# TensorE's order within a slot: the key score ahead of the max score, and the turn of the outputs between them

## The chip, the cores and the metric

One core of a Trainium2 chip runs the whole program. The metric is the device time of one execution in microseconds: 1221.77 us before the change (median of three runs, 1220.28 to 1222.41). Lower is better.

## What is computed

The input is `x`, 8 sequences of 512 tokens with 256 features, float32. Four layers follow each other, each added to its own input:

```
x = x + attn_a(layernorm(x))     # 16 heads of 16, biases, softmax over all 512 keys
x = x + ffn(layernorm(x))        # query, 255 router gates, products along a tree to 256 leaves, leaf values, output
x = x + attn_b(layernorm(x))     # 16 heads of 16, rotary positions, causal softmax
x = x + ffn(layernorm(x))
```

In both attentions `scores = q @ k.T / sqrt(16)`, `softmax(scores) @ v`, and a projection back to 256 features. Every score is wanted twice: once to find the largest of each query's row, and once, less that largest, to be exponentiated.

## The kernel before the change

The work is cut into 16 **phases**: one attention with the feed-forward network behind it, of one of the 8 sequences. Phases 0, 1, 2, 4, 6, 8, 10 and 12 are of `attn_a` ("plain"), phases 3, 5, 7, 9, 11 and 13 to 15 of `attn_b` ("causal"). A phase has 64 **slots**, four for each of 16 steps: a step is a group of four heads and one of four tiles of 128 keys. All engines walk through the same list of slots, and the order on each engine is written out by the program; only semaphores tie them together.

In each slot TensorE (`core` of the tensor block) does this:

- `ahead` calls `scores` (line 1082), the **max score**: 128 queries of one head against its keys (512 in a plain phase; 128, 256, 384 or 512 in a causal one) into one of three banks `ps_max`. It is for the unit that stands 28 slots (LEAD) further on, so that from slot 36 of a phase it belongs to the next phase. VectorE (`largest`, line 842 in a plain phase, 838 in a causal one) reduces the bank to `neg_max`. The max score waits until VectorE has done the reduction three units back, whose bank it takes. The first unit of a phase waits also for the DMAs that stack q and k.
- In slots 9, 25, 41 and 57, `turn_out` (line 1138) transposes the finished output of four heads, four times 128x128, and VectorE (`divide`, lines 863 and 866) divides it by the sums, behind that slot's reduction.
- `by_key` (line 1104), the **key score**: 128 keys against the queries (512, or fewer in a causal phase), with one more row that subtracts the maximum, into one of two banks `ps_key`. ScalarE takes the exponential (line 750). The key score waits until the exponential two slots back is done.
- In every fourth slot `mixed` (line 1128) multiplies the probabilities of four heads with the values, some five slots behind their exponentials. In causal phases GpSimd masks them first (line 655).
- Behind `core` stand the steps due in that slot (`matmul_schedule`): transposes (line 1183) and products (lines 1212 and 1237) of the previous phase's end and of the next phase's start.

VectorE's program goes slot by slot in the same way: first the reduction, then `divide` if there is one, then the steps due (normalisation, line 968; the gates' tree `leaves`, lines 990 to 999; values with bias, line 1045; residual additions, line 900). ScalarE does an exponential per slot, and then its steps. In the first eight slots of phase 0 two max scores are due in each slot (`lead_slots`). Each engine starts its instructions in program order, so one that waits holds all behind it.

The part that the change touches is `core`, with the functions that it calls:

Of the kernel before, what the change touches and what calls it, by code (L numbers as in the profile page):

```python
# [150 lines left out]
def causal(n):  # L151

    return n >= PHASES - AHEAD or (n >= AHEAD and n % 2 == AHEAD % 2)
# [62 lines left out]
def lead_slots(n, slot):  # L216

    if n == 0 and slot < CATCH_UP:
        return 2 * slot - CATCH_UP, 2 * slot - CATCH_UP + 1
    return slot,  # L220
# [24 lines left out]
def out_due(n, slot):  # L245

    if slot % GROUP_SLOTS == (GROUP_SLOTS - GROUP + TURN_LAG) % GROUP_SLOTS and (n > 0 or slot >= TURN_LAG):
        return (slot // GROUP_SLOTS - (1 if TURN_LAG >= GROUP else 0)) % GROUPS
    return None


def work_banks():


    uses = [(step, i, 0, -1) for step, i in PREPARE_FIRST if step in BANK_STEPS]
    for n in range(PHASES + 1):
        for slot in range(-LEAD if n == 0 else 0, SLOTS if n < PHASES else 0):
            if slot >= 0:
                if out_due(n, slot) is not None:
                    uses.append(("turn_out", n, slot))  # L260
                uses += [(step, i, m, n) for step, i, m, part in matmul_schedule(n).get(slot, ()) if part == 0]
    uses.append(("turn_out", PHASES, 0))
    uses += [(step, i, PHASES - 1, PHASES) for step, i in FINISH_LAST if step in BANK_STEPS]
    return {use: at % 2 for at, use in enumerate(uses)}
# [24 lines left out]
def build(nc, x, w, out):  # L289
    with ExitStack() as ctx:  # L290
# [82 lines left out]
        bank_of = {use: ps_work[i] for use, i in work_banks().items()}  # L373
# [681 lines left out]
        def _(pe):  # L1055
            count = Count()
            def take(bank, event):

                if bank.name in count.last_read:
                    read, n = count.last_read[bank.name]  # L1060
                    pe.wait_ge(on[read], count.of(read, count.n[read] - n))
                count.add(event)
                count.last_read[bank.name] = event, count.n[event]
# [21 lines left out]
            def ahead(n, slot):  # L1085
                n, unit, g, j, qt = score_unit(n, slot)
                if n < PHASES:
                    scores(n, unit, g, j, qt)

            def by_key(n, slot):  # L1090
                step, j = slot // GROUP, slot % GROUP
                g, kb = step // TILES, step % TILES
                q0 = P * kb if causal(n) else 0
                if kb == 0 and j == 0:
                    sent = on["shift_sent0"] if g % 2 == 0 else on["shift_sent1"]

                    count.add(f"shift_sent{g % 2}", BLOCKS)
                    pe.wait_ge(sent, count.of(f"shift_sent{g % 2}") * DMA)

                if count.some("exp_done", 1):  # L1100
                    pe.wait_ge(on["exp_done"], count.of("exp_done", 1))
                count.add("exp_done")
                h = GROUP * g + j
                pe.matmul(ps_key[slot % 2][:, 0:T - q0], k_stack[n % 2][0:STACK_ROWS, h, P * kb:P * kb + P],  # L1104
                          q_stack[n % 2][0:STACK_ROWS, h, q0:T], start=True, stop=True).then_inc(on["keyed_full"], 1)

            def mixed(n, step, begun):


                g, kb = step // TILES, step % TILES  # L1110
                q0 = P * kb if causal(n) else 0
                if causal(n):

                    pe.wait_ge(on["causal_done"], count.next("causal_done"))
                else:

                    pe.wait_ge(on["exp_done"], count.of("exp_done", begun))
                if step == 0:

                    pe.wait_ge(on["values_ready"], count.of("values_ready"))  # L1120
                if kb == 0:

                    if count.some("out_ready"):
                        pe.wait_ge(on["out_ready"], count.of("out_ready"))
                    count.add("out_ready")
                for j in range(GROUP):
                    at = VALUE * (HEADS * kb + GROUP * g + j)
                    last = pe.matmul(ps_out[COLS * j:COLS * j + COLS, q0:T], v_flat[n % 2][:, at:at + COLS],  # L1128
                                     probs[step % RING][:, j, q0:T], start=(kb == 0), stop=(kb == TILES - 1),
                                     tile_position=(0, COLS * j))  # L1130
                last.then_inc(on["mixed_done"], 1)

            def turn_out(g, begun, bank):

                pe.wait_ge(on["out_ready"], count.of("out_ready", begun))
                take(bank, "attended")
                for qt in range(TILES):
                    last = pe.transpose(bank[:, P * qt:P * qt + P], out_raw[g % 2][:, P * qt:P * qt + P], ident[:, :])
                last.then_inc(on["out_turned"], 1)

            def core(n, slot):
                for at in lead_slots(n, slot):
                    ahead(n, at)
                if out_due(n, slot) is not None:
                    turn_out(out_due(n, slot), 1, bank_of["turn_out", n, slot])
                by_key(n, slot)
                if slot % GROUP == MIX_LAG % GROUP:
                    step = (slot - MIX_LAG) // GROUP
                    if step >= 0:
                        mixed(n, step, MIX_LAG - GROUP + 1)  # L1150
                    elif n > 0:
                        mixed(n - 1, step + STEPS, MIX_LAG - GROUP + 1)
# [98 lines left out]
            for n in range(PHASES):  # L1251
                due = matmul_schedule(n)
                for slot in range(SLOTS):
                    core(n, slot)
                    for step, i, m, part in due.get(slot, ()):
                        steps[step](m, i, n, bank_of[step, i, m, n], (part,))
# [48 lines left out]
```

## Time and profile before

| | |
|---|---|
| time of the runs, median (lowest to highest) | 1221.77 us (1220.28 to 1222.41) |
| the profiled execution's own time | 1224.61 us |
| its span in the trace | 1222.9 us |
| TensorE matmul busy | 1112.1 us, 91% of the span |
| VectorE busy | 927.2 us, 76% |
| ScalarE busy | 720.2 us, 59% |
| GpSimd busy | 302.7 us, 25% |
| mean granted clock of TensorE | 0.957 of full speed |

Busy time of TensorE is modelled at its ends and matmuls overlap, so the distance from one start to the next tells what a matmul costs in a dense stream. Idle time stands beside an instruction with the engine that ended it, and the chain of waits follows the last instruction back to what released it at each step.

### The profile page before, as it was taken

How to read it: one execution, taken by the hardware profiler on the slowest of the kernel's cores; microseconds unless marked ns; L12 is line 12 of the kernel's file. 1: busy time of each engine (PE TensorE's matmuls, PEld its weight loads, DVE VectorE, ACT ScalarE, POOL GpSimd, SP SyncE). 2: the span in 40 equal slices, each digit the busy share in tenths (PEclk: the TensorE clock that was granted, in tenths of full speed). 3: DMA queues.
4: the chain of work that ended last, by engine and by line, in shares of the span. 5: the costliest groups of instructions: out<-in, count | busy, mean ns of one | idle time of the engine just before them, and what ended most of it. 6: DMA issues, size and time to landing. Idle time of an engine off the chain costs nothing.

```text
span 1222.9 us, 18868 instructions
## 1 busy us (share of the span) xinstructions
PE 1112.1 (91%) x6160; PEld 546.0 (45%) x6160; DVE 927.2 (76%) x2599; ACT 720.2 (59%) x1457; POOL 302.7 (25%) x324
## 2 busy tenths in 40 slices
PE   6589999969999998999999998999999998897986
PEld 3133353434544454444544454444544444443544
DVE  3568778657888879797898869797888867774834
ACT  3056765546647775576747774676747665554551
POOL 3011101321315022331315122331315143261210
PEclk9589999989999999999999999999989999987988
DMA  7322220131403240041403241041402212021000
GB/s 207 65 69 70 63 58 21 35 91 48 105 1 101 74 108 16 18 139 35 104 2 95 79 95 28 19 138 35 105 1 75 83 42 81 1 64 41 19 8 28
DMA packets 67121, 75.33 MB, mean 62 GB/s; under 512 B 12464, under 2 KB 52816, under 8 KB 67024
## 3 DMA queue, kind: packets, MB, share of 16 engines
q1 hardware_dynamic: 66960, 74.09, 22.6%
q8 instruction: 50, 0.82, 0.3%
q14 instruction: 47, 0.39, 0.1%
q0 software_dynamic: 64, 0.03, 0.0%
HBM read 12.45 MB, written 4.19 MB: 14 GB/s over the span
## 4 chain that ended last, share of the span: by engine, by line
PE 55%; DVE 25%; ACT 6%; SPq 5%; issue 4%; DMA 4%; POOL 1%; DVEq 0%; ACTq 0%; POOLq 0%
PE ps_work L1212 12%; PE ps_out L1128 11%; PE ps_max L1082 10%; PE ps_key L1104 9%; PE ps_work L1237 9%; DVE neg_max L842 7%; SPq L492 4%; DVE ps_max L838 4%; DVE scratch L996 3%; PE ps_work L1183 3%; ACT probs L750 2%; DMA q_stack<-q_part 2%; DVE scratch L968 2%; DVE scratch L999 2%; DVE moments L938 1%
## 5 line engine op out<-in xcount | busy, mean ns | idle before, releaser
L750 ACT ACTIVATE probs<-ps_key 128x512 f32<-128x512 f32 (+3 forms) x1024 | 514.4, 518 | 424.2 <-PE ps_key L1104 420.7
L1082 PE MATMUL ps_max<-k_stack,q_stack 96*128 96x512 bf16 (+3 forms) x1024 | 360.3, 355 | 58.2 <-DMA q_stack<-q_part 25.2
L842 DVE TENSOR_REDUCE neg_max<-ps_max 128x1 bf16<-128x512 f32 x512 | 337.1, 683 | 90.5 <-PE ps_max L1082 89.2
L1104 PE MATMUL ps_key<-q_stack,k_stack 97*128 97x512 bf16 (+3 forms) x1024 | 353.5, 348 | 18.6 <-ACT probs L750 12.8
L838 DVE CUSTOM_DVE_ANT_0 ps_max<-ps_max,mask_b 128x128 f32<-128x128 f32 (+3 forms) x512 | 247.7, 502 | 126.4 <-PE ps_max L1082 124.4
L1082 PEld LDWEIGHTS ps_max<-k_stack,q_stack 96*128 96x128 bf16 x1024 | 100.0, 98 | 327.0 <-DVE neg_max L842 121.3
L1128 PE MATMUL ps_out<-probs,v_ones 128*32 128x512 f32 (+3 forms) x2048 | 236.5, 535 | 0.6 <-POOL probs L655 0.6
L655 POOL TENSOR_SCALAR_AFFINE_SELECT probs<-probs 128x512 f32<-128x512 f32 x128 | 82.9, 648 | 462.8 <-ACT probs L750 462.1
L1104 PEld LDWEIGHTS ps_key<-q_stack,k_stack 97*128 97x128 bf16 x1024 | 101.3, 99 | 140.9 <-ACT probs L750 84.6
L1183 PE MATMUL ps_work<-ident,scratch 128*128 128x128 f32 x384 | 65.7, 298 | 21.5 <-DMA a_v_bias<-in_a_v_bias 9.2
L677 POOL TENSOR_TENSOR rstd<-variance,minus_half 128x4 f32<-128x4 f32 (+1 forms) x34 | 33.2, 975 | 209.2 <-DVE variance L951 177.2
L1128 PEld LDWEIGHTS ps_out<-probs,v_ones 128*32 128x32 f32 x2048 | 40.7, 109 | 75.2 <-issue 67.3
L1212 PE MATMUL ps_work<-gate_w,turned_block 128*128 128x255 f32 x256 | 72.8, 412 | 1.4 <-ACT turned_block L771 1.4
L838 DVE DVE_READ_ACCUMULATOR2_ANT neg_max<- 128x1 bf16 x512 | 72.9, 142 | 0.0
L1183 PEld LDWEIGHTS ps_work<-ident,scratch 128*128 128x128 f32 x384 | 48.8, 152 | 47.2 <-DVE scratch L968 23.8
L1212 PE MATMUL ps_work<-leaf_w,turned_block 128*128 128x256 f32 x256 | 66.4, 383 | 1.4 <-ACT turned_block L771 1.4
L771 ACT ACTIVATE turned_block<-ps_work 128x512 f32<-128x512 f32 x96 | 57.3, 598 | 12.6 <-PE ps_work L1183 12.6
L697 POOL TENSOR_TENSOR scratch<-scratch,cosine 128x512 f32<-128x512 f32 x32 | 43.5, 1360 | 66.8 <-ACT scratch L786 35.8
L717 POOL TENSOR_TENSOR k_part<-scratch,k_part 128x512 bf16<-128x512 f32 x32 | 40.3, 1271 | 73.8 <-ACT k_part L808 73.8
L1212 PEld LDWEIGHTS ps_work<-gate_w,turned_block 128*128 128x128 f32 x256 | 52.4, 209 | 12.1 <-ACT turned_block L771 2.0
L1212 PEld LDWEIGHTS ps_work<-leaf_w,turned_block 128*128 128x128 f32 x256 | 46.1, 191 | 11.6 <-ACT turned_block L771 1.9
L717 POOL TENSOR_TENSOR q_part<-scratch,q_part 128x512 bf16<-128x512 f32 x32 | 38.0, 1190 | 40.4 <-ACT q_part L808 40.4
(83 smaller groups left out, 1200.7 us busy)
## 6 DMA issues: line engine op xcount, KB each, us to landing
k_stack<-k_part SPq DMA_DIRECT2D x48, 256.0 KB
q_stack<-q_part SPq DMA_DIRECT2D x48, 256.0 KB
k_stack<-k_part SPq DMA_DIRECT2D x96, 128.0 KB
q_stack<-q_part SPq DMA_DIRECT2D x96, 128.0 KB
x_in<-in_x SPq DMA_DIRECT2D x8, 512.0 KB, 4.1
q_stack<-shift_rows SPq DMA_DIRECT2D x256, 1.0 KB, 1.7
x_again<-in_x SPq DMA_DIRECT2D x8, 512.0 KB, 4.0
x_moved<-x_plain SPq DMA_DIRECT2D x7, 512.0 KB, 3.0
```

The source lines that it names most:

```text
L655: pool.affine_select(out=tile, in_=tile, compare_op=ALU.is_ge, fill=0.0, base=0, pattern=[[0, GROUP], [1, P]], channel_multiplier=-1)\
L717: pool.tensor_tensor(parts[which][2][:, i, :], rest_of(which, m)[:, i, :], parts[which][1][:, i, :], ALU.subtract).then_inc(on["low"], 1)
L750: act.activation(probs[step % RING][:, j, q0:T], ps_key[slot % 2][:, 0:T - q0], ACT.Exp, scale=SCALE).then_inc(on["exp_done"], 1)
L771: act.activation(dst[:, :, 2 * P * i:2 * P * i + 2 * P], bank[:, :].rearrange("p (k n) -> p k n", k=KC), ACT.Copy).then_inc(on["turned"], 1)
L838: dve.tensor_tensor_reduce(out=src, in0=src, in1=mask_b[:, T - keys:], scale=-1.0, scalar=-MASKED, op0=ALU.add, op1=ALU.min, accum_out=dst)\
L842: dve.tensor_reduce(out=dst, in_=src, axis=AX_X, op=ALU.max, negate=True)\
L1082: pe.matmul(dst[:, 0:keys], q_stack[n % 2][0:SPLIT_ROWS, h, P * qt:P * qt + P], k_stack[n % 2][0:SPLIT_ROWS, h, 0:keys], start=True, stop= ...
L1104: pe.matmul(ps_key[slot % 2][:, 0:T - q0], k_stack[n % 2][0:STACK_ROWS, h, P * kb:P * kb + P], q_stack[n % 2][0:STACK_ROWS, h, q0:T], star ...
L1128: last = pe.matmul(ps_out[COLS * j:COLS * j + COLS, q0:T], v_flat[n % 2][:, at:at + COLS], probs[step % RING][:, j, q0:T], start=(kb == 0) ...
L1183: last = pe.transpose(by_tile(bank)[:, k, P * t:P * t + P], src[:, 2 * i + t, P * k:P * k + P], ident[:, :])
L1212: last = pe.matmul(by_tile(bank)[:, t, 0:width], turned[:, k, tile], weight[:, k, 0:width], start=(k == 0), stop=(k == KC - 1))
L1237: last = pe.matmul(bank[:, :], weight[:, k, P * i:P * i + P], turned_heads[:, k, :], start=(k == 0), stop=(k == KC - 1))
```

## The change

Within a slot, TensorE's three parts are put in another order. Nothing else differs: the same instructions, banks, semaphores and waits, and no other engine's program is changed.

```
             def core(n, slot):
+                by_key(n, slot)
+                if out_due(n, slot) is not None:
+                    turn_out(out_due(n, slot), 1, bank_of["turn_out", n, slot])
                 for at in lead_slots(n, slot):
                     ahead(n, at)
-                if out_due(n, slot) is not None:
-                    turn_out(out_due(n, slot), 1, bank_of["turn_out", n, slot])
-                by_key(n, slot)
                 if slot % GROUP == MIX_LAG % GROUP:
```

So a slot that read max score, turn, key score now reads key score, turn, max score; `mixed` and the steps stay behind all three.

## Rows read from the trace of the kernel before

**Rows 1.** The page: busy time of each engine; shares of the chain of waits.
```profile
PE 1112.1 (91%) x6160; PEld 546.0 (45%) x6160; DVE 927.2 (76%) x2599; ACT 720.2 (59%) x1457; POOL 302.7 (25%) x324
...
PE 55%; DVE 25%; ACT 6%; SPq 5%; issue 4%; DMA 4%; POOL 1%; DVEq 0%; ACTq 0%; POOLq 0%
```

**Rows 2.** The page's groups: busy, mean ns; idle before, releaser. Both scores.
```profile
L1082 PE MATMUL ps_max<-k_stack,q_stack 96*128 96x512 bf16 (+3 forms) x1024 | 360.3, 355 | 58.2 <-DMA q_stack<-q_part 25.2
...
L1104 PE MATMUL ps_key<-q_stack,k_stack 97*128 97x512 bf16 (+3 forms) x1024 | 353.5, 348 | 18.6 <-ACT probs L750 12.8
```

**Rows 3.** Busy time by stretch: phase 8 (plain), phase 9 (causal); length, engines, clock.
```profile
639.63:711.32 71.69, 70.27 (x386) 33.73 (x384) 59.98 (x158) 49.89 (x92) 19.81 (x16) 1.00 0.25 74
711.32:777.13 65.81, 61.78 (x386) 32.53 (x385) 55.18 (x166) 39.93 (x91) 17.45 (x22) 1.00 0.25 57
```

**Rows 4.** Timeline of PE, phase 8, slot 3: start us, duration us, instruction.
```profile
643.11 0.38 PE L1082 MATMUL ps_max<-k_stack,q_stack 96*128 96x512 bf16 x1
643.33 0.38 PE L1104 MATMUL ps_key<-q_stack,k_stack 97*128 97x512 bf16 x1
643.55 1.02 PE L1237 MATMUL ps_work<-turned_heads,b_k 128*128 128x512 f32 x2
```

**Rows 5.** Timeline of PE, phase 9, slot 41 and the start of slot 42.
```profile
752.71 0.39 PE L1082 MATMUL ps_max<-k_stack,q_stack 96*128 96x512 bf16 x1
752.94 0.60 PE L1138 MATMUL ps_work<-ident,out_raw 128*128 128x128 f32 x4
753.37 0.27 PE L1104 MATMUL ps_key<-q_stack,k_stack 97*128 97x256 bf16 x1
753.49 0.38 PE L1082 MATMUL ps_max<-k_stack,q_stack 96*128 96x512 bf16 x1
```

**Rows 6.** Chain of waits, phase 9, slots 41 to 52: start, us, what.
```profile
752.78 0.34 PE ps_max L1082
...
764.96 0.61 DVE neg_max L842
...
765.62 0.39 PE ps_max L1082
```

**Rows 7.** Timeline of DVE, phase 9: slot 41's reduction, and two tree steps behind it.
```profile
753.14 0.69 DVE L842 TENSOR_REDUCE neg_max<-ps_max 128x1 bf16<-128x512 f32 x1 [0.64 <-PE ps_max L1082]
...
755.04 0.61 DVE L991 TENSOR_SCALAR scratch<-scratch 128x4 f32<-128x4 f32 x1
...
757.45 0.29 DVE L996 SCALAR_TENSOR_TENSOR scratch<-scratch 128x128 f32<-128x128 f32 x1
```

**Rows 8.** Timeline of PE, phase 9, slot 52, behind the max score.
```profile
765.84 0.33 PE L1104 MATMUL ps_key<-q_stack,k_stack 97*128 97x384 bf16 x1
766.10 0.42 PE L1128 MATMUL ps_out<-probs,v_ones 128*32 128x128 f32 x8
```

**Rows 9.** Timeline of DVE, phase 8, slot 44: one tree step.
```profile
691.80 1.33 DVE L996 SCALAR_TENSOR_TENSOR scratch<-scratch 128x128 f32<-128x128 f32 x1
```

**Rows 10.** Timeline of POOL, phase 8, the same time.
```profile
691.72 1.27 POOL L662 TENSOR_TENSOR x_again<-x_again,a_o_bias 128x512 f32<-128x512 f32 x1 [3.81 <-DMA x_again<-in_x]
```

**Rows 11.** Chain of waits, phase 8, slots 9 to 27: its first and last lines.
```profile
650.79 0.34 PE ps_max L1082
...
671.38 0.61 DVE neg_max L842
...
672.03 0.39 PE ps_max L1082
```

**Rows 12.** Timeline, phase 9: DVE's reduction of slot 23, PE's transposes of slot 31.
```profile
735.86 0.70 DVE L838 CUSTOM_DVE_ANT_0 ps_max<-ps_max,mask_b 128x512 f32<-128x512 f32 x1 [0.56 <-PE ps_max L1082]
...
742.99 0.63 PE L1183 MATMUL ps_work<-ident,scratch 128*128 128x128 f32 x4 [0.62 <-DVE v_ones L1045]
```

**Rows 13.** Timeline of PE, phase 9, slot 35.
```profile
745.12 0.38 PE L1082 MATMUL ps_max<-k_stack,q_stack 96*128 96x512 bf16 x1
745.62 0.39 PE L1104 MATMUL ps_key<-q_stack,k_stack 97*128 97x512 bf16 x1
```

## The prediction

> **What bounds the kernel now.** I read the page first, for which engine carries the chain of waits; then the two scores' groups, for what TensorE waits for; then single phases by stretch; then TensorE's, VectorE's and ScalarE's timelines beside the chain, slot by slot, in phase 8 (plain) and phase 9 (causal). Phases 3 to 11 repeat these two, so they stand for nine phases.
>
> TensorE is busy for 91% of the span and carries 55% of the chain, VectorE 25% [rows 1]. A plain phase takes 71.7 us and a causal one 65.8 us, both at full granted clock [rows 3]. In a dense stretch the next matmul starts 0.22 us behind either score of 512 columns [rows 4], however long the bars are; so TensorE streams without a hole for most of a phase, and what can be won or lost is the little it waits. The two scores' own idle time is 58.2 and 18.6 us, 25.2 of it for the stacking DMAs [rows 2]. The waits sit in a few places per phase, the same ones each time. In most the chain runs: a max score starts a reduction, VectorE then works without pause for 12 to 21 us, and TensorE waits for its last reduction in front of another max score [rows 6, 11]. I call that a VectorE stretch. Each begins where VectorE stood idle for a max score (0.64 us in [rows 7]) and ends where TensorE stands idle for VectorE.
>
> **The change part by part.** Nothing is added or removed: 1024 key scores, 1024 max scores and 64 turns stay. Relative to `mixed` and the steps, whose place stays, a key score starts earlier by the max score's stream (0.22 us, less in a causal unit) and by the turn where there is one; a max score starts later by the key score's stream and the turn's. In a dense stream that is no time at all. It counts only at the waits, and there two rules decide. Where a stretch both begins and ends at a max score, its end moves back with its beginning, and TensorE gains only one key score's stream, which it now does ahead of the wait instead of behind it. Where TensorE waits in front of a key score for ScalarE, the max score that was done ahead of that wait now stands behind it.
>
> First, slot 41. VectorE waits for its max score there, in 13 phases the last time before the gates' tree. In phase 9 the max score starts at 752.71 and the turn at 752.94; the turn ends where the key score starts, 753.37, which costs 0.12 [rows 5]. In the new order key score and turn stand in front: 0.12 + 0.43 = 0.55 us later. VectorE's program still has the reduction first and `divide` behind it, so the early turn helps nothing and the whole stretch to slot 52 moves by 0.55 us. TensorE gains the key score of slot 52: between 765.84 and 766.10 lie 0.26 us, of which 0.09 is the change to `mixed`'s small weights that stays, so 0.17 [rows 8]. Net +0.38 us. In phase 8 both key scores have 512 columns, 0.22 us [rows 4]: 0.22 + 0.43 - 0.22 = +0.43 us.
>
> A part is given back. In slot 44 of phase 8 a tree step of VectorE takes 1.33 us [rows 9] where the same step takes 0.29 in phase 9 [rows 7]; it starts 0.08 us behind a GpSimd addition that a DMA has released and that ends at 692.99 [rows 10]. It is held until then, and an end set by a DMA does not move with VectorE: a VectorE that comes 0.65 us later is held for less. Bounds: nothing given back, or all the 1.04 us of the hold. The reductions, which I see not stretched, take most of the time just before; I take 0.26 us. In phase 9 a tree step of 4 columns takes 0.61 us [rows 7] beside GpSimd's masking; at most those 0.61 are given back or as much is met anew; I take 0.20. So the slot 41 stretch is worth +0.17 us in a plain phase and +0.18 in a causal one.
>
> The Trainium skill (SBUF — State Buffer, "Who interferes with whom") says why: a VectorE instruction with two SBUF inputs and a GpSimd instruction that reads SBUF exclude each other, and whichever comes second waits for the whole of the first. Rows 9 and 10 agree (1.33 us, ending 0.14 us behind the addition). By that rule alone a moved VectorE can lose the hold wholly, which is my third case below; without a hold to lose, slot 41 would stay at +0.43.
>
> Second, slot 9 of the five plain phases 4 to 12. There too the max score feeds VectorE, and the chain stays on VectorE from 651 to 672.03 [rows 11]; its later reductions and normalisations are still late at slots 31 and 32. The max score comes 0.22 + 0.43 = 0.65 us later. TensorE meets this at slot 25 (where ScalarE waits for a result of that stretch), 27, 31 and 32. Behind slot 32 the key score is hidden and the max score is not waited for longer than the transposes of slot 31, so 0.65 less at most 0.22 and at least nothing: I take +0.50. In causal phases VectorE is idle again between slot 9 and its next work, and nothing comes of it.
>
> Third, slot 23 of causal phases. VectorE waits 0.56 us for that max score, and TensorE 0.62 us for VectorE at the transposes of slot 31 [rows 12]. The key score put in front has 384 columns, 0.17 us as in slot 52 [rows 8]; nothing is hidden at the far end, since the transposes stand behind both scores in either order. +0.17 us.
>
> Fourth, waits for ScalarE. In slot 35 of phase 9 the max score starts at 745.12 and the key score at 745.62 [rows 13], so 0.50 less its stream of 0.22 is a wait, and the max score was done in its cover. Now it stands behind: +0.22, less what ScalarE gains by earlier key scores, which is 0 to 0.22 according to what fed it. In causal phases transposes feed ScalarE there: +0.17; the same pattern in slot 18 with a narrower max score: +0.10. In plain phases key scores feed it: +0.05 for both.
>
> Sum for one phase: plain 0.17 + 0.50 + 0.05 = 0.72 us; causal 0.18 + 0.17 + 0.27 = 0.62. Phases 3 to 11 are four plain and five causal: 2.9 + 3.1 = 6.0 us. Phases 1, 2, 13 and 14 have the slot 41 stretch, 0.7 together. Phase 12 has slot 9 but begins its tree behind a DMA, so it keeps the gain of 0.22: +0.3. In phase 0 the double max scores no longer hold up the key scores, but VectorE is waiting for its first input rows then; I take 0. The long waits for stacked q and k at slot 36 now come behind a key score (-0.2 each, three of them), and the work that feeds those DMAs on VectorE starts as much later: 0. In phase 15, from slot 36 on, there is no max score, so nothing changes. Together +7.0 us, within bounds worked out below. Against the profiled execution that is 1224.61 + 7.0 = 1231.6; that execution lies 2.8 us above the median, and from the median I get 1221.77 + 7.0 = 1228.8 us.
>
> **The rivals.** Case A, this forecast: +4 to +9 us.
>
> Case B, the delays add up in full. Nothing of the GpSimd holds is given back, and slot 9's stretch is paid whole. Plain 0.43 + 0.65 + 0.05 = 1.13, causal 0.38 + 0.17 + 0.27 = 0.82; 4 x 1.13 + 5 x 0.82 = 8.6; four more slot 41 stretches at 0.4 and phase 12 at 0.65: 2.3. +11, 1232.8 us. For it: the chain enters VectorE at the moved max score each time [rows 6, 11]. Against it: a fixed end such as that of rows 10 absorbs.
>
> Case C, the holds go. The plain tree step falls from 1.33 to 0.29 us and the causal one from 0.61: plain 0.72 + 0.26 - 1.04 = -0.06, causal 0.62 + 0.20 - 0.61 = +0.2; with the rest about +1, 1222.8 us, no change that can be told. For it: both holds begin within tenths of a microsecond of the moved time. Against it: GpSimd's addition takes 1.27 us, more than VectorE moves.
>
> Case D, the other side: the key score in the cover of the waits. If VectorE makes up its later start before it becomes late, each VectorE stretch keeps only its gain of one key score. It decides at one point: whether VectorE is idle or held for 0.55 us less than before between slots 42 and 46. Two stretches in 14 phases by 0.22 us: -6 us, 1215.6 us. For it: exponentials come earlier at every turn, and 1.04 us of hold lie there in plain phases. Against it: the causal stretch has almost nothing idle from 753.14 to 765.57 [rows 6].
>
> **How the numbers follow.** A 0.42, B 0.20, C 0.20, D 0.18. The time is A's, 1228.8 us. A's own range is 1225.8 to 1230.8. The range that should hold the time 8 times in 10 takes in C and B and reaches more than halfway from C to D: 1218.5 to 1234.5. No change means within 0.2% (2.4 us), which is about what a measurement of this kernel can tell. A and B are slower, 0.62; C is the same, 0.20; D is faster, 0.18.
>
> **What would show it.** In the changed kernel's trace of phases 8 and 9, VectorE's idle time in front of slot 41's reduction grows by the key score and the turn (1.2 us instead of 0.64 in phase 9), and the max score of slot 52 comes 0.3 to 0.7 us later behind the phase's start, the key score of slot 52 ahead of it. In slot 35 of phase 9 the key score waits and the max score stands behind it. Phase 9 takes about 66.4 us and phase 8 about 72.4. Case C shows in the step of rows 9 at 0.3 us; case D in phases shorter than 71.5 and 65.6 us. I am wrong in kind if VectorE's idle time before slot 41 grows and slot 52 does not move, or if the distance from one start to the next in dense stretches [rows 4] is not 0.22 us any more, since then the order costs by itself.

## The result, and the profile after

The changed kernel takes 1228.92 us (median of 9 runs, 1224.98 to 1234.34) against 1221.12 us (9 runs): 1.007 times the time before, 95% interval 1.0046 to 1.0095. It is slower, by 7.8 us; 7.0 were forecast. (The kernel before came out 0.65 us lower over 9 runs than over the three that the forecast started from.) The profiled execution took 1227.48 us, with a span of 1225.8.

The page of the changed kernel, the lines that answer to [rows 1, 2]:

```profile
PE 1107.2 (90%) x6160; PEld 548.7 (45%) x6160; DVE 920.1 (75%) x2599; ACT 723.0 (59%) x1457; POOL 301.9 (25%) x324
...
PE 57%; DVE 25%; ACT 6%; issue 6%; SPq 2%; DMA 2%; POOL 0%; DVEq 0%; ACTq 0%; POOLq 0%
...
L1082 PE MATMUL ps_max<-k_stack,q_stack 96*128 96x512 bf16 (+3 forms) x1024 | 357.5, 353 | 47.0 <-DMA q_stack<-q_part 22.1
L1104 PE MATMUL ps_key<-q_stack,k_stack 97*128 97x512 bf16 (+3 forms) x1024 | 358.4, 352 | 34.1 <-ACT probs L750 27.8
```

Idle time ahead of the max scores fell from 58.2 to 47.0 us, and ahead of the key scores it rose from 18.6 to 34.1. The wait for VectorE has a key score in its cover now, and the wait for ScalarE no longer has a max score in it. The page does not tell the rest. Phases 8 and 9 by stretch, as in [rows 3]:

```profile
640.77:713.88 73.11, 69.91 (x385) 33.57 (x384) 59.85 (x157) 50.39 (x93) 19.34 (x16) 1.00 0.25 73
713.88:779.94 66.06, 62.73 (x386) 33.93 (x385) 54.46 (x165) 39.87 (x91) 17.67 (x22) 0.97 0.25 57
```

The plain phase is longer by 1.42 us and the causal one by 0.25. (0.16 of that belongs to the edges: a phase is cut at its first key score, which now stands first. Counted from the phase's first score, it is 1.26 and 0.40.) Slot 41 of phase 9, TensorE and then VectorE, against [rows 5, 7]:

```profile
755.97 0.28 PE L1104 MATMUL ps_key<-q_stack,k_stack 97*128 97x256 bf16 x1
756.09 0.60 PE L1138 MATMUL ps_work<-ident,out_raw 128*128 128x128 f32 x4
756.53 0.38 PE L1082 MATMUL ps_max<-k_stack,q_stack 96*128 96x512 bf16 x1
```

```profile
756.95 0.69 DVE L842 TENSOR_REDUCE neg_max<-ps_max 128x1 bf16<-128x512 f32 x1 [1.17 <-PE ps_max L1082]
...
758.84 0.17 DVE L991 TENSOR_SCALAR scratch<-scratch 128x4 f32<-128x4 f32 x1
```

The max score starts 0.56 us behind the slot's first score, where it was the first. VectorE's idle time is 1.17 us where it was 0.64. But the tree's step of line 991 takes 0.17 us where it took 0.61: the mask of GpSimd is not beside it any more. The chain of waits still runs from slot 41's max score over VectorE to slot 52's [rows 6], and the key score of slot 52 stands ahead of the wait [rows 8]:

```profile
756.69 0.23 PE ps_max L1082
...
768.25 0.61 DVE neg_max L842
...
768.91 0.39 PE ps_max L1082
```

```profile
768.46 0.33 PE L1104 MATMUL ps_key<-q_stack,k_stack 97*128 97x384 bf16 x1
768.91 0.39 PE L1082 MATMUL ps_max<-k_stack,q_stack 96*128 96x512 bf16 x1
769.23 0.42 PE L1128 MATMUL ps_out<-probs,v_ones 128*32 128x128 f32 x8
```

In phase 8 the tree is still held, one level of the tree earlier than in [rows 9, 10]. VectorE's and GpSimd's timelines:

```profile
694.27 1.29 DVE L996 SCALAR_TENSOR_TENSOR scratch<-scratch 128x64 f32<-128x64 f32 x1
```

```profile
694.22 1.27 POOL L662 TENSOR_TENSOR x_again<-x_again,a_o_bias 128x512 f32<-128x512 f32 x1 [3.71 <-DMA x_again<-in_x]
```

And phase 8 lost 0.87 us already in slots 15 to 18, where I had forecast 0.05. TensorE's timeline there, and ScalarE's ahead of it:

```profile
660.14 0.38 PE L1104 MATMUL ps_key<-q_stack,k_stack 97*128 97x512 bf16 x1 [0.69 <-ACT probs L750]
660.36 0.38 PE L1082 MATMUL ps_max<-k_stack,q_stack 96*128 96x512 bf16 x1
```

```profile
658.88 0.63 ACT L808 ACTIVATE k_part<-scratch 128x512 bf16<-128x512 f32 x1 [0.56 <-DVE scratch L1026]
```

ScalarE stood idle for 0.56 us for a result of VectorE's stretch that begins in slot 9. Before, it did not wait there. So ScalarE inherits slot 9's delay, and TensorE takes it over from ScalarE at a key score, with the max score behind.

### The profile page after: what moved, and what is told of

Read it like the earlier page. It is cut to its first block, busy times and chain, and to the rows that moved or that the text cites. A ratio compares the mean times of both kernels' runs of the same rounds, so it can differ in the third digit from the quotient of the medians.

```text
span 1225.8 us, 18868 instructions
## 1 busy us (share of the span) xinstructions
PE 1107.2 (90%) x6160; PEld 548.7 (45%) x6160; DVE 920.1 (75%) x2599; ACT 723.0 (59%) x1457; POOL 301.9 (25%) x324
## 4 chain that ended last, share of the span: by engine, by line
PE 57%; DVE 25%; ACT 6%; issue 6%; SPq 2%; DMA 2%; POOL 0%; DVEq 0%; ACTq 0%; POOLq 0%
PE ps_work L1212 13%; PE ps_key L1104 11%; PE ps_out L1128 11%; PE ps_max L1082 9%; PE ps_work L1237 7%; DVE neg_max L842 6%; DVE ps_max L838 3%; ACT probs L750 3%; PE ps_work L1183 3%; DVE scratch L996 3%; DVE scratch L999 2%; DVE scratch L968 2%; PE ps_work L1138 2%; DVE scratch L1026 2%; DMA q_stack<-q_part 2%
## 5 line engine op out<-in xcount | busy, mean ns | idle before, releaser
L1104 PE MATMUL ps_key<-q_stack,k_stack 97*128 97x512 bf16 (+3 forms) x1024 | 358.4, 352 | 34.1 <-ACT probs L750 27.8
```

## The experiments

Theory T is the prediction's: the loss comes in at waits, above all since key score and turn stand ahead of the max scores that feed VectorE in slots 9 and 41. Theory R is its rival: the max scores have lost the cover of ScalarE's waits. All kernels start from the one before; the diffs are to it, `M`, `T` and `K` stand for its three parts (max score, turn, key score), and all were timed in 5 rounds with it on the same chip. Ratios are to the kernel before.

**e1, e2, e3, e4: which slots, and which part.**

```
 e1   core(n, slot):  M T K in the four turn slots,  K T M elsewhere
 e2   core(n, slot):  K T M in the four turn slots,  M T K elsewhere
 e3   core(n, slot):  K M T everywhere
 e4   core(n, slot):  K T M if slot in 26..32 or 42..56,  M T K elsewhere
```

> The new order in 60 slots of a phase, and the old one (max score, turn, key score) in the four slots with a turn. Theory T (the time is lost because key score and turn, 0.55 to 0.66 us, now stand ahead of the max score that feeds VectorE in slots 9 and 41, and ScalarE and TensorE inherit that start): VectorE's idle time ahead of slot 41's reduction falls back from 1.17 to 0.64 us in phase 9 and from 1.51 to 1.07 in phase 8, phase 8 falls from 73.1 to 72 us or less, and the program takes 1217 to 1222 us, since the gain of a hidden key score at slots 27 and 52 stays. Theory R (the time is lost because the max scores no longer stand in the cover of the waits for ScalarE, in slots 15 to 18, 35 and 43, none of which has a turn): those slots are as in the changed kernel, so 1227 to 1230 us.

> The reverse: the old order in 60 slots, and the new one (key score, turn, max score) in the four slots with a turn. T: the whole loss and none of the gain: VectorE's idle time ahead of slot 41 grows by the same 0.44 to 0.53 us, phase 8 takes 73.0 us or more, 1227 to 1233 us. R: nothing is changed in the slots that wait for ScalarE, so 1220 to 1223 us.

> Key score, max score, turn in every slot: the change without the turn ahead of the max score. T: the max score of slots 9 and 41 comes later by the key score alone (0.12 to 0.22 us), which the hidden key score at the end of the stretch pays back: phase 8 72.0 us, phase 9 65.7, 1219 to 1224 us. R: the max scores stand out of cover as in the changed kernel: 1227 to 1230 us.

> The new order only where TensorE waits for VectorE ahead of a max score, slots 26 to 32 and 42 to 56, none with a turn; the old order elsewhere, so that no stretch of VectorE begins later than before. T: the pure gain, a key score of 0.17 to 0.22 us hidden at the end of two stretches in 13 phases, less 0.22 for slot 43's wait for ScalarE: 1216 to 1220 us. R: slots 35 and 15 to 18 keep their cover, slot 43 loses it in plain phases, and nothing is gained: 1221 to 1223 us.

| | ratio, 95% interval | median | phase 8 | phase 9 |
|---|---|---|---|---|
| e1, turn slots old | 0.9997 (0.9981 to 1.0012) | 1219.94 | 71.97 | 65.95 |
| e2, turn slots only | 1.0061 (1.0038 to 1.0083) | 1227.99 | 72.76 | 66.06 |
| e3, turn last | 1.0006 (0.9987 to 1.0026) | 1221.63 | 72.39 | 65.67 |
| e4, ends only | 0.9953 (0.9935 to 0.9972) | 1215.16 | 71.34 | 65.79 |

The phases of e1 and e3 are cut at a key score that stands first, as in the changed kernel. Counted from the phase's first score, e1 is 0.12 and 0.28 us above the kernel before, and e3 0.53 and 0.02.

All four came out on T's side, e4 0.8 us below T's own range, and e2's phase 8 0.24 below the 73.0 that T wanted. The new order in 4 of 64 slots costs what the whole change costs, and in the other 60 it costs nothing. With the turn behind both scores the loss is gone too, so it is the turn ahead of the max score. Where TensorE waits for VectorE the new order pays: e4 is 0.47% faster than before. The rows of e4 for phases 8 and 9:

```profile
634.87:706.21 71.34, 69.97 (x386) 33.57 (x384) 60.02 (x158) 49.80 (x92) 19.81 (x16) 1.00 0.25 75
706.21:772.00 65.79, 61.66 (x386) 32.99 (x385) 55.37 (x166) 39.73 (x91) 17.59 (x22) 1.00 0.25 57
```

In plain phases it saves 0.35 us. In causal ones it saves 0.02, since GpSimd's masking comes about 1 us earlier there and meets another step of the tree. VectorE's step and GpSimd's masking in e4, phase 9:

```profile
753.65 0.85 DVE L999 SCALAR_TENSOR_TENSOR scratch<-scratch 128x256 f32<-128x256 f32 x1
```

```profile
753.42 0.81 POOL L655 TENSOR_SCALAR_AFFINE_SELECT probs<-probs 128x512 f32<-128x512 f32 x1 [2.95 <-ACT probs L750]
```

That step takes 0.42 us in the kernel before, where the masking lies beside the next step of line 996 instead (0.94 us, in e4 0.68). 0.43 less 0.26 is 0.17 us that VectorE comes later, and that takes back the hidden key score.

The rows do not carry e4's whole gain. Over phases 3 to 11 its phases are shorter by some 2 us, leaving out what the clock cost phases 5 and 11 of the kernel before; its median is 4.5 us lower and its ratio stands for 5.7. No run tells where the rest comes from.

**e5, e6, e7: one place at a time.**

```
 e5   core(n, slot):  K T M if slot in 15..18 or 33..36,  M T K elsewhere
 e6   core(n, slot):  K T M if slot == 9,   M T K elsewhere
 e7   core(n, slot):  K T M if slot == 41,  M T K elsewhere
```

> The new order only in slots 15 to 18 and 33 to 36, where TensorE waits for ScalarE ahead of a key score; the old order elsewhere, turns included. It prices the part of the prediction on waits for ScalarE by itself. Theory T (what counts is whether a max score that stood in the cover of a wait now stands behind it, and who feeds ScalarE): causal phases +0.27 us as predicted (0.10 at slot 18, 0.17 at slot 35), plain phases between +0.05 (key scores feed ScalarE) and +0.44 (something else does: both waits cost a max score), so phase 8 71.7 to 72.1 us, phase 9 66.1 us, and the program 1221 to 1226 us with a median before of 1220. Theory R2 (the 0.87 us that phase 8 loses at slots 15 to 18 in the changed kernel is due to the order in these slots, not to slot 9): phase 8 loses 0.8 us or more here.

> The new order in slot 9 alone. T: VectorE begins 0.65 us later there and stays late to slot 32, and ScalarE, which takes VectorE's results in slots 12 to 14, inherits 0.65: phase 8 loses 0.65 us by slot 18 and ends at 72.2 to 72.5 us; causal phases, where VectorE is idle again in slot 13, stay at 65.8. The program loses 3 to 5 us: 1223 to 1225 with a median before of 1220. R2: slot 9 costs nothing by itself, phase 8 stays at 71.7 and the program at 1220.

> The new order in slot 41 alone. The prediction's first step without its gain at slot 52. T: phase 8 loses 0.65 us less what GpSimd's hold gives back (0.14 measured in the changed kernel, 0.26 predicted), 72.1 to 72.2 us; phase 9 loses 0.55 less 0.2 to 0.5 given back, 65.9 to 66.2 us; the program 1223 to 1227 us with a median before of 1220. If the holds had been lost wholly (case C), phase 8 would be no slower than 71.7.

| | ratio, 95% interval | median | phase 4 | phase 8 | phase 9 |
|---|---|---|---|---|---|
| e5, ScalarE's waits | 1.0017 (1.0002 to 1.0032) | 1222.03 | 72.13 | 70.74 | 66.19 |
| e6, slot 9 | 1.0028 (1.0015 to 1.0041) | 1223.12 | 72.38 | 72.38 | 65.97 |
| e7, slot 41 | 1.0028 (1.0014 to 1.0041) | 1223.02 | 72.13 | 72.22 | 65.91 |

The three places cost 0.17, 0.28 and 0.28%, 0.73% together, each within some 0.15%; the change costs 0.70%. That the two agree does not show that the parts add. The change also has the new order in e4's slots, which gained 0.47%, and so by adding it should cost 0.26%. In the same way e1, which has the slots of e4 and e5, should gain 0.30% and gained 0.03%. The places are shown one by one; what they are worth together depends on what they meet, as on a hold that the changed kernel's trace shows ("A hold that no case had", below). The first row below is e6's VectorE at slot 9, the second its ScalarE behind it:

```profile
650.26 0.69 DVE L842 TENSOR_REDUCE neg_max<-ps_max 128x1 bf16<-128x512 f32 x1 [1.50 <-PE ps_max L1082]
```

```profile
655.97 0.63 ACT L808 ACTIVATE k_part<-scratch 128x512 bf16<-128x512 f32 x1 [0.53 <-DVE scratch L1026]
```

VectorE was idle for 0.84 us there before and is for 1.50 now, and the start of slot 18's product, counted from the phase's start, moves by 0.64 us. In e5 it moves by 0.22, one max score. 0.64 + 0.22 is the changed kernel's 0.87: both theories hold there, in two terms that add. R2 is refuted, which wanted 0.8 or more in e5. In phase 9 e5 costs 0.38 us: 0.17 at slot 18, 0.22 at slot 35.

e7 costs 0.53 us in phase 8 and 0.09 in phase 9 (counted at slot 52), out of 0.66 and 0.55 that VectorE begins later. In phase 9 the step of line 991 takes 0.16 us, and so gives back 0.45:

```profile
753.16 0.69 DVE L842 TENSOR_REDUCE neg_max<-ps_max 128x1 bf16<-128x512 f32 x1 [1.19 <-PE ps_max L1082]
...
755.06 0.16 DVE L991 TENSOR_SCALAR scratch<-scratch 128x4 f32<-128x4 f32 x1
```

**e8, e9: GpSimd's hold on the tree.** e8 has the old order, e9 the new one.

```
-                if slot == 40 and not causal(n):
+                if slot == 56 and not causal(n):
                     load_again(n)
```

> The kernel before, its order unchanged, with the load of x for the residual (which releases GpSimd's addition) issued at slot 56 of a plain phase instead of slot 40. It takes the hold out of the gates' tree. If the addition holds VectorE's step of 1.33 us in slot 44 (theory T), that step takes 0.29 us, slot 52 comes up to 1.04 us earlier in plain phases and they last 70.7 to 71.2 us; 8 plain phases, so the program takes 1212 to 1217 us with a median before of 1220. If the 1.33 us have another cause (theory H), nothing changes in that step, and the program stays at 1219 to 1221 us.

> The changed kernel with the residual's load at slot 56, so that GpSimd's addition is out of the gates' tree. T (the change and the hold are separate terms, and the hold gave back 0.14 us of slot 41's delay in plain phases): the load saves what it saved in the old order (0.63%) less that 0.14 us in 8 phases, so the ratio to the kernel before is 1.000 to 1.003, 1220 to 1224 us with a median before of 1220. If the hold covered most of the change's cost (theory H2), the ratio would stay at 1.005 or more.

e8 takes 1212.76 us, 0.9937 (0.9919 to 0.9954). The step of [rows 9] takes 0.30 us, and phase 8 is 1.04 us shorter:

```profile
685.63 0.30 DVE L996 SCALAR_TENSOR_TENSOR scratch<-scratch 128x128 f32<-128x128 f32 x1
```

```profile
633.46:704.11 70.65, 69.55 (x385) 33.96 (x384) 58.94 (x158) 49.71 (x92) 19.80 (x16) 1.00 0.25 76
```

So the addition held it, and the hold was on the path. e9 takes 1220.78 us, 1.0016 (0.9999 to 1.0033); the forecast was 1.000 to 1.003. Phase 8 is 72.04 us in it, 1.07 less than in the changed kernel, whose phases are cut in the same way: the new order moves the hold to another step of the tree and does not lose it.

**e10, e11, e12: the gains together.** All three have the late load.

```
 e10  core(n, slot):  K T M if slot in 26..32 or 42..56,  M T K elsewhere
 e11  core(n, slot):  K M T if slot in 26..32 or 42..56,  M K T elsewhere
 e12  core(n, slot):  M K T everywhere
```

> Both gains together: the new order in slots 26 to 32 and 42 to 56 alone, and the residual's load at slot 56. T: ends alone gave 0.9953 and the load alone 0.9937; where the hold is gone TensorE waits less for VectorE in slots 47 to 52 of plain phases, but one wait at the end remains and hides one key score: 0.988 to 0.992, 1206 to 1211 us with a median before of 1220. If the two gains are the same wait removed twice: 0.993 to 0.995.

> As the kernel with both gains, and the turn stands behind both scores in every slot (max, key, turn in the old order's slots). T: the turn was nowhere ahead of a max score in that kernel, so VectorE gains nothing; the key score of slots 9, 25, 41 and 57 comes 0.43 us earlier, which helps only where TensorE waits for ScalarE soon after (slots 25 and 43 of plain phases, up to 0.25 us each, ahead of a VectorE wait that ends at the same time as before). So within 0.2% of it, 0.987 to 0.992. A theory that the turn costs by standing anywhere ahead of a score expects 4 x 0.2 us per phase, 0.98.

> Max score, key score, turn in every slot, with the residual's load at slot 56: the order of before but for the turn, and no key score put ahead of a max score anywhere. It tells what the new order in slots 26 to 32 and 42 to 56 is still worth when the hold is gone. The two single gains (0.47% and 0.63%) gave 0.6% together. If they were one wait removed twice, this kernel takes as little as the one with the new order there, 0.991 to 0.9945 of before. If the new order at the ends still pays by itself, as it did in slots 27 and 52 of the old kernel, this one stays at 0.995 or more.

| | ratio, 95% interval | median | phase 8 | phase 9 |
|---|---|---|---|---|
| e10, ends and late load | 0.9940 (0.9921 to 0.9960) | 1211.91 | 70.57 | 65.79 |
| e11, and the turn last | 0.9924 (0.9902 to 0.9946) | 1210.39 | 70.63 | 65.52 |
| e12, old order, turn last, late load | 0.9949 (0.9933 to 0.9965) | 1215.83 | 71.03 | 65.76 |

e10 missed: I expected 0.988 to 0.992. Its phase 8 is only 0.08 us shorter than e8's, since without the hold TensorE hardly waits for VectorE in slots 47 to 51 and there is little left to cover. The gains of e4 and e8 were in good part one wait removed twice. Against e8, which has the late load alone (0.9937), e10 gains nothing that can be told, and e11 too little to part the two (0.9902 to 0.9946 and 0.9919 to 0.9954). e11 has the lowest time of all, 0.76% under the kernel before, just outside the range expected for it (0.987 to 0.992), and 1.5% under the changed one. Against e12 it saves 0.40 us in phase 8 and 0.24 in phase 9, but the intervals of the two ratios overlap, and e12's own phase 8 is 0.38 us longer than e8's. So that the new order at the ends still pays without the hold is shown against e12's order only, and in single profiles.

Against e10 the turn behind the key score saves 0.27 us in phase 9. I had called it worth nothing, and missed its way. The exponentials come earlier there, so GpSimd's masking does too, and VectorE's step of line 991 is no longer beside it. VectorE's row in e10, then in e11:

```profile
747.10 0.61 DVE L991 TENSOR_SCALAR scratch<-scratch 128x4 f32<-128x4 f32 x1
```

```profile
746.06 0.16 DVE L991 TENSOR_SCALAR scratch<-scratch 128x4 f32<-128x4 f32 x1
```

The masking starts 0.01 us ahead of VectorE's step of line 990 in e10 and 0.35 ahead in e11. The step of line 990 takes 0.16 us longer in e11, the one of line 991 0.45 less, and VectorE, which is nowhere idle by more than 0.05 us between slots 42 and 52, is 0.27 us earlier from slot 43 on.

## Why the prediction was right, and where it was not

The side and the mechanism hold: key score and turn ahead of the max scores of slots 9 and 41 make the loss. That the time fits to 0.12 us (1228.8 forecast, 1228.92 measured) is in part luck, for the split between the phases was wrong and its errors cancel (below, "The sum"). The terms, each as the runs give it per phase; they interact and do not add up to a phase:

| step of the prediction | forecast | measured |
|---|---|---|
| slot 41, plain: net of the key score gained | +0.17 us | +0.31 (slot 40 to 52 of the changed kernel); e7: 0.53 - 0.22 |
| slot 41, causal: net | +0.18 | -0.13; e7: 0.09 - 0.17 |
| slot 9, plain | +0.50 | +0.65 (e6) |
| slot 9, causal | 0 | +0.15 (e6) |
| slot 23, causal | +0.17 | +0.17 |
| ScalarE's waits, plain | +0.05 | +0.22 (e5) |
| ScalarE's waits, causal | +0.27 | +0.38 (e5) |

- **Slot 41.** That the end of the stretch moves with its beginning is shown by e7, and that one key score is gained there by the rows of slot 52. What the holds give back was sized wrongly both ways: in plain phases 0.13 us of 0.66, not 0.26, for the hold met VectorE again one step earlier; in causal ones 0.46 of 0.55, not 0.20, for the masking was missed wholly. Case C's mechanism was therefore nearly right for the causal phases, and case A's for the plain ones.
- **Slot 9.** The mechanism is right and the reach was longer than I saw. I had ScalarE inherit the delay only at slot 25. It inherits it at slots 12 to 14 already, by the wait for line 1026's result; in causal phases the exponential of slot 12 starts 0.21 us later in e6. In the prediction the plain phases' key scores "feed" ScalarE at slots 15 to 18; the rows show that VectorE does. That is the step that failed, by 0.82 us in slot 18 of phase 8; but 0.65 of it is slot 9's own term, met there and not again later.
- **Slots 18 and 35.** A max score out of cover costs its whole stream when ScalarE is not fed by earlier key scores: 0.22 us (plain, slot 18), 0.17 and 0.22 (causal). In plain phases slot 35 costs nothing, as forecast.
- **The sum.** For a plain and a causal phase together 1.34 us were forecast, and 1.67 measured. Counted from the phases' first scores, the four plain phases 4 to 10 lost 0.86 to 1.26 us each, 4.1 together, where 2.9 were forecast (0.72 each). The causal phases 3, 7 and 9 lost 0.40 to 0.42 each, which makes 2.0 for five, where 3.1 were forecast (0.62 each). The sum of 6.1 against 6.0 is two errors that cancel. The plain phases were sized too low at ScalarE's waits, at slot 9 and by a hold that the prediction did not see (the next point); the causal ones too high at slot 41, where the masking gave back 0.46. Phase 15, put at nothing, took 0.95 us more (52.46 and 53.41): key score and turn change places there too. Over phases 3 to 11 the profiled executions give less, because phases 5 and 11 of the kernel before took 67.4 and 66.8 us instead of the 65.8 of phases 3, 7 and 9, with the clock lower (below). That its profile was 2.9 us shorter in span than the changed one's, and not 7.8, is in good part due to this; the medians and their interval are what counts.
- **Case D** named the point that decides (VectorE less idle or held by 0.55 us between slots 42 and 46), and in causal phases it nearly came about. e4 shows the gain behind it: put where it covers a wait and feeds none, the same swap is 0.47% faster.

- **A hold that no case had.** Phases 4 and 8 are of one kind and lose 1.02 and 1.42 us. TensorE's slots part between 22 and 25, and the trace shows why. VectorE's rows of line 1012 (two inputs in SBUF) in phases 4 and 8, then GpSimd's of line 717:

```profile
386.10 0.68 DVE L1012 TENSOR_TENSOR scratch<-scratch 128x512 f32<-128x512 f32 x1
...
663.96 1.71 DVE L1012 TENSOR_TENSOR scratch<-scratch 128x512 f32<-128x512 f32 x1
```

```profile
386.11 1.68 POOL L717 TENSOR_TENSOR k_part<-scratch,k_part 128x512 bf16<-128x512 f32 x1
...
663.97 1.15 POOL L717 TENSOR_TENSOR k_part<-scratch,k_part 128x512 bf16<-128x512 f32 x1
```

The two start 0.01 us apart in both phases. In phase 4 GpSimd was held (1.68 us), in phase 8 VectorE (1.71), and phases 6 and 10 go as phase 8 does. In the kernel before the same step took 1.12 us in either phase. Behind it TensorE is 0.46 us later in phase 8 than in phase 4 at slot 25, and 0.40 at the phase's end. So the new order brings two instructions to a tie there, and VectorE lost it in three of four phases. The prediction looked for holds in the gates' tree alone.

## What to carry to other kernels

Swapping two instructions of an engine without idle time costs nothing by itself: look for the waits, and ask of each which of the two is done in its cover, and whose start feeds the engine that is late next. An instruction that feeds the bottleneck's partner should stand first in its slot, ahead of anything nobody waits for soon; the other one should be put first only where the engine is about to wait. When a delay is forecast, list the fixed ends it will run into (a transfer, another engine's instruction), since those give back anything between none and nearly all of it. And look for new ones that the delayed engine comes to meet: one such tie was worth 0.4 us of a phase here, and the effects of single places did not add.

## What was not expected of the hardware

**A hold can turn on 0.1 us.** In e5 phase 8 came out 0.95 us shorter than before, though the order in its first slots costs 0.22. VectorE's step of line 1026 (two inputs in SBUF) and GpSimd's of line 717 meet in slot 22. VectorE's row in e5, then GpSimd's:

```profile
667.32 0.67 DVE L1026 TENSOR_TENSOR scratch<-scratch,q_part 128x512 f32<-128x512 f32 x1
```

```profile
667.36 2.76 POOL L717 TENSOR_TENSOR q_part<-scratch,q_part 128x512 bf16<-128x512 f32 x2 [3.58 <-ACT q_part L808]
```

VectorE starts 0.04 us ahead and takes 0.67 us. In the kernel before it starts 0.10 behind and takes 1.60:

```profile
667.10 1.60 DVE L1026 TENSOR_TENSOR scratch<-scratch,q_part 128x512 f32<-128x512 f32 x1
```

```profile
667.00 1.15 POOL L717 TENSOR_TENSOR q_part<-scratch,q_part 128x512 bf16<-128x512 f32 x1 [3.43 <-ACT q_part L808]
```

This is what the Trainium skill says (SBUF — State Buffer, "Who interferes with whom"): whichever of the two comes first has the shared pair for its whole length. These rows agree, 0.67 against 1.60 us. Phase 10 of the same execution saved as phase 8 did. Phases 4 and 6 did not: phase 4 took 72.13 us, 0.49 more than before, so e5's plain cost is 0.22 us at slot 18 and up to 0.49 by the phase's end.

**The clock falls in the same place in some phases.** TensorE's granted clock was 1.00 in phase 9 of the kernel before, and fell in slot 52 of phase 5 to the lower of its two levels (0.50 from 489 to 492 us, which is 1.2 GHz). The stretch behind slot 52 in phase 5 and in phase 9, in the kernel before (the third number from the right is the clock):

```profile
489.50:494.40 4.90, 4.90 (x32) 2.53 (x32) 3.67 (x7) 3.39 (x8) 0.43 (x1) 0.72 0.00 0
766.40:771.30 4.90, 4.90 (x41) 2.94 (x35) 4.36 (x10) 3.77 (x10) 0.64 (x1) 1.00 0.02 4
```

At a mean of 0.72 TensorE got through 32 matmuls in 4.9 us, and through 41 at 1.00. What TensorE had done before was the same in both: slots 46 to 52, with five waits of 0.28 to 0.82 us for VectorE in 7 us. Slot 52 still came at the same time in both phases; by slot 55 phase 5 was 1.55 us behind. In the changed kernel the mean clock was 0.97 in phases 3, 7 and 9 and they took 66.06 us as phases 5 and 11 did at 1.00, so there it cost nothing. Why it falls in one phase and not in its like, no run shows. Much of the spread between executions of one kernel, 6 us here, looks to be this; that is argued from single profiles, and not shown.
